# Softplus summed on TensorE, a sixth drive on GpSimd, and preparation groups in adjoining steps

## The reference, cut to what matters

```
xz = x_seq @ W_in;  x, z = xz[..., :192], xz[..., 192:]
x  = silu(causal_conv(x, conv_w, conv_b))
proj = x @ W_xproj
dt = softplus(proj[..., :6] @ W_dt + b_dt)
h  = exp(dt[:, :, None] * A) * h + dt[:, :, None] * B[:, None, :] * x[:, :, None]   # for each token
y  = einsum('bds,bs->bd', h, C) + x * D
out = (y * silu(z)) @ W_out
```

## Time and profile before

| | |
|---|---|
| median of 3 runs | 5625.2 us (5623.45 to 5625.22) |
| the profiled execution | 5622.07 us, its span 5620.2 us |
| VectorE busy | 5265.8 us (94% of the span) |
| GpSimd busy | 4899.0 us (87%) |
| TensorE busy | 4417.3 us (79%), mean granted clock 0.753 of full speed |
| ScalarE busy | 3184.7 us (57%) |

### The profile page before, as it was taken

The page is one execution under the profiler, slowest core; times in us unless marked ns, Lnnn a source line. Parts: engine busy times, 40 slices in busy tenths (PEclk is TensorE's granted clock), DMA queues, the critical chain, the costliest instruction groups (busy, mean ns, idle before and its releaser), DMA issues. The chain is left out here.

```text
span 5620.2 us, 74988 instructions
## 1 busy us (share of the span) xinstructions
PE 4417.3 (79%) x17412; PEld 1176.0 (21%) x17412; DVE 5265.8 (94%) x3821; ACT 3184.7 (57%) x5221; POOL 4899.0 (87%) x2361
## 2 busy tenths in 40 slices
PE   6878577778878787788887887878778887788887
PEld 4553111111111111111111111111111111111111
DVE  5556499999999999999999999999999999999997
ACT  2237455555555566555666555665555566655564
POOL 0020299999999999999999999999999999999998
PEclk9999776667777777777777777777777777777777
DMA  2238555556656556666656665666665665666666
GB/s 75 76 92 241 164 189 184 186 183 200 212 191 202 196 196 197 207 193 209 191 194 196 204 204 198 196 196 197 202 208 189 206 194 194 198 206 198 205 193 200
DMA packets 365955, 1062.74 MB, mean 189 GB/s; under 512 B 71396, under 2 KB 119926, under 8 KB 315340
## 3 DMA queue, kind: packets, MB, share of 16 engines
q1 hardware_dynamic: 355724, 1045.89, 57.8%
q10 hardware_dynamic: 8064, 14.16, 0.8%
q0 software_dynamic: 1984, 1.06, 0.1%
HBM read 849.20 MB, written 211.63 MB: 189 GB/s over the span
## 5 line engine op out<-in xcount | busy, mean ns | idle before, releaser
L1464 POOL TENSOR_TENSOR hc<-hring,c_rep 128x1024 f32<-128x1024 f32 x1541 | 3599.4, 2358 | 73.1 <-DVE hring L1419 69.6
L1419 DVE TENSOR_TENSOR_SCAN hring<-decay,carry,u_ps 128x1024 f32<-128x1024 f32 x1221 | 2833.8, 2346 | 0.0
L1170 PE MATMUL u_ps<-stack_b,w_spread 48*128 48x512 bf16 x2442 | 992.4, 495 | 1008.6 <-DVE hring L1419 1003.7
L1401 DVE TENSOR_TENSOR u_ps<-u_ps,u_rep 128x1024 f32<-128x1024 f32 x1221 | 1491.7, 1222 | 69.0 <-DMA u_rep<-u_scr 52.9
L1295 ACT ACTIVATE decay<-dt_rep,w_a 128x1024 f32<-128x1024 f32 x1222 | 1396.4, 1145 | 221.2 <-DVE hring L1419 208.1
L1188 PE MATMUL y_ps<-hc,w_gather 128*32 128x512 f32 x6144 | 1131.2, 818 | 0.0
L1295 ACT ACTIVATE u_ps<-dt_rep,w_a 128x1024 f32<-128x1024 f32 x322 | 359.3, 1116 | 1104.2 <-DVE hring L1419 1103.9
L1451 POOL TENSOR_TENSOR drive_p<-u_rep,b_rep 128x1024 f32<-128x1024 f32 x322 | 759.5, 2359 | 10.7 <-DMA u_rep<-u_scr 10.7
L1419 DVE TENSOR_TENSOR_SCAN hring<-u_ps,carry,drive_p 128x1024 f32<-128x1024 f32 x321 | 755.7, 2354 | 0.0
L1170 PEld LDWEIGHTS u_ps<-stack_b,w_spread 48*128 48x128 bf16 x2442 | 144.8, 100 | 2371.0 <-DVE hring L1419 2166.7
L1211 PE MATMUL prep_ps<-xn,w_conv 128*128 128x512 f32 x792 | 476.6, 749 | 27.2 <-DMA xn<-xn_scr 25.5
(11 more groups left out here) (148 smaller groups left out, 4044.3 us busy)
## 6 DMA issues: line engine op xcount, KB each, us to landing
dt_rep<-dt_scr SPq DMA_DIRECT2D x194, 1024.0 KB, 5.9
u_rep<-u_scr SPq DMA_DIRECT2D x194, 1024.0 KB, 8.0
c_rep<-bc_scr SPq DMA_DIRECT2D x260, 512.0 KB, 4.9
b_rep<-bc_scr SPq DMA_DIRECT2D x130, 512.0 KB, 4.3
xn<-xn_scr SPq DMA_DIRECT2D x132, 384.0 KB, 5.4
y_scr<-y_sb SPq DMA_DIRECT2D x768, 64.0 KB, 2.0
xn<-xn_scr SPq DMA_DIRECT2D x132, 256.0 KB, 4.7
dt_scr<-dt_sb SPq DMA_DIRECT2D x260, 128.0 KB, 2.1
```

Source lines behind the costliest of these rows:

```text
L1170: mm = nc.tensor.matmul(u_ps[nv % NSLOT][:, sl], w["spread"][:, q, :], upper(stack_b[drv][:, sl]), start=True, stop=True)
L1401: nc.vector.tensor_tensor(slot[:, :], slot[:, :], u_rep[r][:, b, :], ALU.mult).then_inc(drive_ready, 1)
L1419: nc.vector.tensor_tensor_scan(hring[nv % NHR][:, ::step], factor[:, ::step], term[:, ::step], carry[:, drv, nv:nv + 1], ALU.mult, ALU.add ...
L1464: nc.gpsimd.tensor_tensor(hc[nv % NHC][:, :], hring[nv % NHR][:, :], c_rep[q][:, :], ALU.mult).then_inc(c_applied, 1)
```

## The change

GpSimd's drives go from 5 to 6 in a pass. The sum inside softplus leaves GpSimd: TensorE adds `soft` and `dt_sb` with two identity matmuls for each of three groups of 512 columns into `prep_ps`, and ScalarE copies each sum into `dt_sb`; `prep_out` then counts ten copies in a pass instead of seven, and `dt_ready` is gone. The dt groups stand in steps 3, 4, 5, the sums in 7, 8, 9, the convolution groups in 18, 19, 20. The slice's sums stand at 10 and 12 and its projection at 13. Some loads and stores move by a step or two.

```diff
-POOL_UNITS = (2, 6, 11, 15, 19)
+POOL_UNITS = (2, 6, 10, 14, 18, 22)
-        NPREP = 7
+        NPREP = 10
-        LOW_AT = 2
-        DT_AT = (4, 6, 8)
-        CONV_AT = ((14, 14, 14), (16, 16, 16), (18, 18, 18))
-        SUM_AT = (7, 9)
-        U_AT = (8, 10)
+        LOW_AT = 1
+        DT_AT = (3, 4, 5)
+        CONV_AT = ((18, 18, 18), (19, 19, 19), (20, 20, 20))
+        SUM_AT = (7, 8, 9)
+        U_AT = (10, 12)
-        FIRST_LOAD_AT = 12
+        FIRST_LOAD_AT = 13
-        B_AT = (11, 7)
+        B_AT = (11, 13)
-        U_STORE_AT = (11, 13)
+        U_STORE_AT = (12, 14)
-        SLICE_AT, Z_AT = 15, (20, 22)
-        SUM_Y_AT, PROJECT_AT, RES_AT, OUT_STORE_AT = (0, 10), 12, 13, 14
+        SLICE_AT, Z_AT = 15, (21, 22)
+        SUM_Y_AT, PROJECT_AT, RES_AT, OUT_STORE_AT = (10, 12), 13, 14, 15
...
-                    if n % 8 == 4:
-                        load_u(*later(4, u, n, it, dr))
+                    if n % 8 == 5:
+                        load_u(*later(3, u, n, it, dr))
...
                 def prep(m, pn, it, dr, slicing):     # SP
-                            made, free = ready(2 * pn + h + 1, UNITS * (pn - 1))
-                            sp.wait_ge(dt_ready, made)
+                            made, free = ready(NPREP * pn + 9 + h, UNITS * (pn - 1))
+                            sp.wait_ge(prep_out, made)
...
                 def prep(m, pn, it, dr, slicing):     # TensorE, low
-                            pe.wait_ge(gated, 2 * (pn - 1 - OUT_LAG) + 1)
+                            pe.wait_ge(z_out, 2 * (pn - OUT_LAG))
...
+                    if m in SUM_AT:
+                        g = SUM_AT.index(m)
+                        pe.wait_ge(prep_out, NPREP * pn + 7 + g)
+                        pe.wait_ge(soft_step, 2 * (2 * pn + g // 2) + 2)
+                        nc.tensor.matmul(prep_ps[:, :], w["ident"][:, :], soft[:, PART[g]], start=True, stop=False)
+                        nc.tensor.matmul(prep_ps[:, :], w["ident"][:, :], dt_sb[:, PART[g]], start=False, stop=True).then_inc(prep_done, 1)
...
                 def slice_out(m, k, it, dr):          # TensorE
-                                pe.wait_ge(z_out, 2 * (k + 1))
+                                pe.wait_ge(prep_out, NPREP * (k + OUT_LAG + 2))
                             else:
-                                pe.wait_ge(prep_out, NPREP * (k + OUT_LAG + 2))
+                                pe.wait_ge(gated, 2 * k + 1)
...
+                    if m - 1 in SUM_AT:               # ScalarE
+                        g = SUM_AT.index(m - 1)
+                        act.wait_ge(prep_done, NPREP * pn + 8 + g)
+                        nc.scalar.copy(dt_sb[:, PART[g]], prep_ps[:, :]).then_inc(prep_out, 1)
...
                     for h in range(2):                # GpSimd
-                        if m == SUM_AT[h]:
-                            pool.wait_ge(soft_step, 2 * (2 * pn + h) + 2)
-                            nc.gpsimd.tensor_tensor(dt_sb[:, HALVES[h]], soft[:, HALVES[h]], dt_sb[:, HALVES[h]], ALU.add).then_inc(dt_ready, 1)
                         if m == U_AT[h]:
-                            pool.wait_ge(dt_ready, 2 * pn + h + 1)
+                            pool.wait_ge(prep_out, NPREP * pn + 9 + h)
```

More of the change, by code:

```diff
@@ L823, in scan @@
         soft_step = sem("soft_step")
-        dt_ready = sem("dt_ready")
         u_ready = sem("u_ready")
@@ L1148, in _ @@
                 dt_loads = (UNITS * LAST + LEAD + 4) // 8 + 1
-                u_loads = (UNITS * LAST + LEAD + 3) // 8 + 1
+                u_loads = (UNITS * LAST + LEAD + 2) // 8 + 1
                 for r in range(2):
```

## The result

| | before | after |
|---|---|---|
| median | 5625.15 us (5623.45 to 5625.22) | 5770.68 us (5765.95 to 5771.9) |
| ratio | | 1.0259, 95% interval 1.0244 to 1.0274 |
| profiled span | 5620.2 us | 5770.0 us |

The account below looks back on a forecast made before the run. VectorE was taken as the bound. Lateness of 64 x (2.3 + 0.2 + 0.2 + 0.15) plus 56 x 0.3, together 199 us, less 71.7 gained, on 5622.07 gave 5749.6, rounded to 5750 us; range 5550 to 5860.

Parts of the forecast that it names:

- The bound: Whole pass: VectorE ends every pass with no gap to lose, busy 999.31 us in a thousand.
- group 2 behind ScalarE's copy: Steps 20 to 21: some 3.5 us in a room of 3.37, so 0.2 us late; ends 0 and 0.5.
- low: Steps 0 to 2: low, moved to step 1 on TensorE, meets a low clock; 0.2 us late a pass.
- The term of group 0: Steps 18 to 20: first convolution group begins at 1.2 GHz, takes 4.82 us; drive 2.3 us late, ends -0.1 and 2.9.
- The sums at steps 8 to 10: Softplus sums on TensorE: 9.1 us in a room of 8.99, 0.15 us late; ends 0 and 2.9.
- the projection: Step 13, in 56 passes: waits for a gate VectorE finishes late; 0 or 1.2 us late, taken as 0.3.
- the range's lower end: Forecast's own range, group 0 early and the small terms nothing: 5665 us.
- The signs: If right: unit 3 waits about 2.3 us, VectorE busy 96 to 97%, group 0 about 4.9 us, GpSimd waiting 4 to 5%.
- The first (the clock holds): TensorE reaches step 18 at 2.4 GHz, everything fits and the whole drive is gained: 5553 us; chance 0.20.
- the third rival: Low clock stays through low, dt and the sums too: 6047 us if in every pass, 5900 taken; chance 0.12.
- GpSimd's and SP's terms of nothing: GpSimd's moved products and SP's moved store and load cost nothing; upper ends 2.31 and 1 us a pass.

Follow-up runs that it names:

- the fast version: The changed kernel with convolution groups at steps 14, 16, 18 and the slice's second sum at step 11 instead of 12; 5562.28 us, ratio 0.9886 against the kernel before.
- the fast version with five drives: The fast version with GpSimd's drives cut to five, at units 2, 6, 11, 15, 19; 5773.09 us, ratio 1.0261 against the kernel before.

## Why the prediction was right

**Right, with its size.** The bound, the place (unit 3, steps 18 to 20), the cause (the clock down after the light steps 14 to 17) and the sign were as predicted. So were the two small terms beside it: group 2 behind ScalarE's copy, forecast 0.2, measured 0.18 us; low, forecast 0.2, measured 0.26.

**Mis-sized.** The term of group 0 was taken as 4.82 us from start to start, and the drive as 2.3 us late; the group took 5.42 (5.49 in its row), and the drive was 2.97 late in the passes with an output slice. 0.60 of the 0.67 us is the group, the rest the hand-overs. That is the upper end which the prediction gave (5.41 and 2.9). The 4.82 was one pass of the earlier trace rows; slow first groups of the kernel before took from 4.09 to 5.48 us, by where in the group the clock comes back. In the changed kernel the passes settle on one length, and the clock comes back only at the group's end. In the eight passes before the first slice, group 0 took 4.25 and 5.47 us by turns, so 4.82 was fair there as a mean. This is 0.67 x 56 = 38 us more than forecast.

**Not there.** The sums at steps 8 to 10 (0.15) and the projection (0.3) cost nothing: 26 us less than forecast. The projection's wait of 2.07 us is in the trace as worked out, but its room sufficed as the clock held through it. It became real, up to 1.4 us a pass, as soon as the first stall was taken away.

**Left out.** The lead-in, 9 us between the two profiles. The corrections, 38 - 26 + 9, leave the 21 us between 5750 and 5771. That it is not more is in part luck, as errors of opposite sign stand in the sum.

**Slips in its sums.** The terms of steps 20 to 21 add to 3.6 us, not 3.5, which still gives 0.2; those of steps 8 to 10 leave 0.1, where 0.15 was taken; the range's lower end comes to 5669 by its own sum, not 5665. None moves the forecast by more than 4 us.

**The signs.** VectorE was busy 95.9% (96 to 97 was said), and group 0 stood at 5.49 us, not at about 4.9. GpSimd waited for scans 2.4% of the span (139 us), not 4 to 5; another 133 us it waited for TensorE's state sums.

**The rivals.** The first (the clock holds) was decided at step 18 as said, and against it. Its argument from the earlier trace rows was weaker than it reads: the median of 593 ns is of groups 0 and 1 together, and group 0 alone ran at the full clock in 28 of 66 cases.

By the Trainium skill's page "TensorE: Matmul & The Clock Gate" ("Why this matters for your kernels") throughput is kept when no idle gap between bursts is longer than about 3 us. The prediction called the gaps of steps 14 to 17 short by that rule, but step 15 has no spread, and the gap before step 16's spread is 3.24 us. The clock was down behind it (the granted clock is 0.50 from 3023 to 3035), which the page would have. But it was 0.50 from 3022 to 3023 already, so it fell before TensorE, done with the state sum at 3020.11, had been idle for 2 us. At steps 0 and 1 of the same pass the changed kernel does not agree with the page:

```profile
3051.25 0.62 PE L1171 MATMUL u_ps<-stack_b,w_spread 48*128 48x512 bf16 x2 [2.57 <-DVE hring L1431]
3053.49 1.03 PE L1171 MATMUL u_ps<-stack_b,w_spread 48*128 48x512 bf16 x2 [1.62 <-DVE hring L1431]
```

The second spread ran slow after gaps of 2.57 and 1.62 us.

The price of this rival, 5553, was reached to within 9 us by the fast version, though with the convolution groups apart. Of the third rival the low clock came in part (in the pass shown the third dt group took 1.97 us and the first softplus sum 3.19 us), but no drive waited there. GpSimd's and SP's terms of nothing held: after the first drive no drive or scan waited for GpSimd or for a load.

## What to carry to other kernels

Before packing work into adjoining steps of an in-order queue, add up what stands between two instructions that the bounding engine waits for, at the clock that the steps *before* leave; here the group behind the light stretch took 5.49 us instead of 2.84. Taking one stall away can expose another that it covered, so give each place its own room (here a gate one step ahead of its user) and do not price it by the trace in which it is hidden. And which units an engine is given changes when other engines' queues are released: compare such sets in place, not by their number.

## What the runs showed of the hardware that was not expected

Passes settle on one length, or on a short cycle of lengths. From the eleventh on, every pass of the changed kernel took 78.50 or 78.51 us, from the start of its first scan to that of the next. From the thirteenth on so did every pass of the fast version with five drives, though its waits are at units 13, 9 and 16 instead of 3. TensorE of that version, in order of time:

```profile
2999.52 2.08 PE L1249 MATMUL prep_ps<-soft,w_ident 128*128 128x512 f32 x2
...
3078.02 1.22 PE L1249 MATMUL prep_ps<-soft,w_ident 128*128 128x512 f32 x1
```

The change with five drives settled on 81.92 us. Other versions repeat a cycle: 77.67 and 79.34 us by turns with the convolution right behind the projection, and in the kernel before five passes of 76.15 or 76.16 us and one of 76.63.

One reading is that a stall that hangs on where the clock is switched moves the pass until the switches fall at the same places again, after one pass or after a few. The stall is then not averaged over all places, as the 0.67 us above show. That the switching fixes the length I only infer; no run tried it by itself.
